# Attention and experts on one core: wavelength weights folded into the row sums at the PSUM copy, stores queued behind loads, output bias added early

## The reference, cut to what is computed

```python
xn = layernorm(x)                                   # (16, 256, 128)
Q, K, V = heads(xn @ Wq + bq), heads(xn @ Wk + bk), heads(xn @ Wv + bv)   # 16 heads of 8
for wl in range(16):                                # wavelengths
    m = cos(phase_modulators[wl])                   # one number a head
    s = (Q * m) @ (K * m).T / sqrt(8)
    s = s * cos(2.7e-12 * s * s)
    acc += (softmax(s) @ V) * interference_weights[wl]
attn = (acc / 16) @ Wo + bo
ffn = top-1 routed experts of xn, each with 640 slots: relu(t @ w1 + b1) @ w2 + b2, times the gate's probability
out = x + attn + ffn
```

## Time and profile before

| | us |
|---|---|
| median of 3 runs (all: 1810.4, 1809.99, 1807.09) | 1809.99 |
| the profiled execution, its own time | 1809.65 |
| its span, first to last instruction | 1807.9 |
| ScalarE busy in the span | 1726.9 (96%) |
| VectorE busy | 1526.0 (84%) |
| TensorE busy | 1490.7 (82%) |
| GpSimd busy | 157.6 (9%) |
| mean granted TensorE clock | 0.986 |

### The profile page before, as it was taken

How to read it: one execution, slowest core, us unless ns; L and a number is a source line. 1 busy time by engine, 2 the same in 40 slices (tenths; PEclk the granted TensorE clock), 3 DMA queues, 4 the chain that set the end, 5 groups by cost and what they waited for, 6 DMA issues and landing times. The chain is left out here.

```text
span 1807.9 us, 45710 instructions
## 1 busy us (share of the span) xinstructions
PE 1490.7 (82%) x20014; PEld 942.5 (52%) x20014; DVE 1526.0 (84%) x2554; ACT 1726.9 (96%) x533; POOL 157.6 (9%) x168
## 2 busy tenths in 40 slices
PE   4797888777899999999997787777787787778877
PEld 2364544544556666656664454444455555445555
DVE  8445887889898888988888999999988998898785
ACT  3699999999999999999999999999999999999995
POOL 6200111110000000000000131332000000000000
PEclk9799999999999999999999999999999999999998
DMA  6000111000011110111000000000000000000001
GB/s 207 21 15 15 37 49 43 23 25 15 22 36 42 42 43 20 31 36 43 22 22 15 18 12 25 23 25 19 15 2 15 15 15 15 15 15 2 8 13 31
DMA packets 44999, 50.07 MB, mean 28 GB/s; under 512 B 6725, under 2 KB 37359, under 8 KB 44799
## 3 DMA queue, kind: packets, MB, share of 16 engines
q1 hardware_dynamic: 42463, 42.91, 7.5%
q0 software_dynamic: 2048, 4.20, 0.7%
q10 hardware_dynamic: 288, 0.00, 0.0%
HBM read 30.96 MB, written 15.73 MB: 26 GB/s over the span
## 5 line engine op out<-in xcount | busy, mean ns | idle before, releaser
L1044 ACT ACTIVATE Pr<-T 128x4096 f32<-128x4096 f32 x482 | 1694.3, 3626 | 17.7 <-PE bank L924 16.9
L924 PE MATMUL bank<-Pr,Vst 128*32 128x256 f32 x15424 | 936.7, 383 | 249.6 <-ACT Pr L1044 140.9
L924 PEld LDWEIGHTS bank<-Pr,Vst 128*32 128x32 f32 x15424 | 520.2, 110 | 546.8 <-issue 343.8
L866 DVE COPY T<-bank 128x512 f32<-128x512 f32 x252 | 172.4, 684 | 82.9 <-PE bank L860 82.9
L850 DVE TENSOR_REDUCE negmax<-bank 128x2 f32<-128x512 f32 x256 | 164.1, 681 | 30.1 <-PE bank L844 28.7
L1015 PE MATMUL bank_b<-terms,ident 128*128 128x128 f32 x1024 | 150.3, 280 | 0.8 <-DVE terms L1003 0.7
L965 DVE SCALAR_TENSOR_TENSOR d_mantissa<-d_mantissa 128x1024 f32<-128x1024 f32 x108 | 147.0, 1361 | 0.0
L968 DVE SCALAR_TENSOR_TENSOR shared<-shared,d_scaled 128x1024 f32<-128x1024 f32 x108 | 140.0, 1297 | 0.0
L1015 PEld LDWEIGHTS bank_b<-terms,ident 128*128 128x128 f32 x1024 | 130.3, 192 | 16.0 <-issue 9.1
L971 DVE SCALAR_TENSOR_TENSOR shared<-d_mantissa,shared 128x1024 f32<-128x1024 f32 x108 | 132.0, 1222 | 2.9
L963 DVE SCALAR_TENSOR_TENSOR shared<-d_mantissa 128x1024 f32<-128x1024 f32 x108 | 130.9, 1212 | 0.0
(11 more groups left out here) (175 smaller groups left out, 911.1 us busy)
## 6 DMA issues: line engine op xcount, KB each, us to landing
Ks<-qk_parts SPq DMA_DIRECT2D x31, 288.0 KB
Qs<-qk_parts SPq DMA_DIRECT2D x93, 96.0 KB
work<-in_L_ffn_w_dram SPq DMA_DIRECT2D x16, 256.0 KB, 3.5
qk_parts<-Pr SPq DMA_DIRECT2D x8, 384.0 KB, 2.7
qk_parts<-work SPq DMA_DIRECT2D x8, 384.0 KB, 2.8
dispatched<-T SPq DMA_DIRECT2D x5, 512.0 KB, 4.9
region<-dispatched SPq DMA_DIRECT2D x8, 320.0 KB, 3.5
expert_out<-work SPq DMA_DIRECT2D x8, 320.0 KB, 2.4
```

Of the source, the lines that this page charges most:

```text
L866: nc.vector.tensor_copy(T[par][:, ds(p * BANK, BANK)], sc_bank[rr][:, :]).then_inc(sc_read, 1)
L924: ins = nc.tensor.matmul(bank[VC * j:VC * (j + 1), half * SEQ:(half + 1) * SEQ], Vst[par][:, at:at + VC], moving, start=opens and half == ...
L1044: nc.scalar.activation(Pr[n % RING][:, :], T[par][:, :], ACT.Exp, scale=scales[u % 2][w]).then_inc(exp_done, 1)
```

## The change

There are four parts.

1. A tile `row_weight` (128 x 6, one column a group) is set to 16 by GpSimd, and 16 DMAs on ScalarE's queue then write the 16 wavelengths' weights to the rows of sums, four partitions each. At the end of the setup VectorE takes its reciprocal, `row_scale`.
2. The copy of a group's bank (`dve_products`) becomes a product with that column of `row_scale`: the value rows are divided by 16, the sums by their weight. The reciprocal of a turned sum then holds the weight already, and the operation that formed `gain` is gone, with one wait of VectorE on itself.
3. In SP's order the loads of units 3 and 4 (for units 5 and 6) are issued ahead of the last store of the unit before. The wait for all stores moves with the last one, behind the loads for unit 6.
4. The four additions of the output bias move from `pool_combine` to the beginning of GpSimd's plain path, behind the staging of the first two units.

```diff
+    FIRST_OF = (0, 3, 6, 8, 11, 14)
+    LAST_OF = (2, 5, 7, 10, 13, 15)
...
-        gain = sb("gain", [P, SLOTS, OTW])
+        row_weight = sb("row_weight", [P, len(FIRST_OF)])
+        row_scale = sb("row_scale", [P, len(FIRST_OF)])
...
                 def _(pool):
+                    pool.memset(row_weight[:, :], float(W)).then_inc(weight_room, 1)
                     pool.memset(one_col[:, :], 1.0).then_inc(root_table, 1)
...
                     act.dma_start(bk_s[:, :], bk.rearrange("(d a) -> d a", a=1)).then_inc(bias_in, 16)
+                    act.wait_ge(weight_room, 1)
+                    for w in range(W):
+                        q = GROUP_OF[w]
+                        row = (w - FIRST_OF[q]) * OC + HD
+                        act.dma_start(row_weight[row:P:VC, q:q + 1], weights.rearrange("(a w) -> a w", a=1)[:, w:w + 1].to_broadcast([GR, 1])
+                                      ).then_inc(row_weight_in, 16)
...
                     link(nc.vector.tensor_copy(flag[:, :], one[:, 3:4]))
+                    dve.wait_ge(row_weight_in, 16 * W)
+                    nc.vector.reciprocal(row_scale[:, :], row_weight[:, :])
...
+            def pool_output_bias(pool):
+
+                pool.wait_ge(xn1_ready, SIDE_TILES)
+                for c in range(CHUNKS):
+                    b = base[:, c * CH:(c + 1) * CH, :]
+                    nc.gpsimd.tensor_tensor(b, b, bo_s[:, :].unsqueeze(1).to_broadcast([P, CH, D]), ALU.add).then_inc(biased, 1)
...
             def pool_combine(pool, c):
 
                 s = slice(c * CH, (c + 1) * CH)
-                nc.gpsimd.tensor_tensor(base[:, s, :], base[:, s, :], bo_s[:, :].unsqueeze(1).to_broadcast([P, CH, D]),
-                                        ALU.add).then_inc(pool_comb, 1)
+                pool.wait_ge(biased, CHUNKS)
                 pool.wait_ge(gathered[c], 16 * CH)
                 nc.gpsimd.tensor_tensor(got[:, s, :], got[:, s, :], over(r[:, 0, s], D), ALU.mult).then_inc(pool_comb, 1)
-                pool.wait_ge(pool_comb, 2 * (c + 1))
+                pool.wait_ge(pool_comb, c + 1)
                 nc.gpsimd.tensor_tensor(base[:, s, :], base[:, s, :], got[:, s, :], ALU.add).then_inc(base_ready, 1)
...
-                nc.vector.tensor_copy(pv_s[q % 2][:, :], pv_bank[q % 2][:, :]).then_inc(pv_copied, 1)
+                nc.vector.tensor_scalar(pv_s[q % 2][:, :], pv_bank[q % 2][:, :], row_scale[:, q:q + 1], None, ALU.mult).then_inc(pv_copied, 1)
...
                 nc.vector.reciprocal(rsum[:, 0:size, :].unsqueeze(3), slots[:, :, :, HD:OC]).then_inc(inverted, 1)
                 dve.wait_ge(inverted, n + 1)
-                nc.vector.tensor_tensor(gain[:, 0:size, :], rsum[:, 0:size, :], weight, ALU.mult).then_inc(gain_ready, 1)
-                dve.wait_ge(gain_ready, n + 1)
                 if n >= 2:
                     dve.wait_ge(terms_summed, n - 1)
                 nc.vector.tensor_tensor(terms[n % 2][:, 0:size, :].rearrange("p s (a d) -> p s a d", d=HD), slots[:, :, :, 0:HD],
-                                        gain[:, 0:size, :].unsqueeze(3).to_broadcast([P, size, OTW, HD]), ALU.mult).then_inc(terms_ready, 1)
+                                        rsum[:, 0:size, :].unsqueeze(3).to_broadcast([P, size, OTW, HD]), ALU.mult).then_inc(terms_ready, 1)
...
                     stage_v(pool, u, u)
+                pool_output_bias(pool)
...
-                for u in range(2, 4):
+                for u in range(2, 5):
                     j = (u - 2) * NQ_SIDE
                     sp.wait_ge(sc_made, pair_no(u, 0))
                     load_stack(sp, u + 2, u % 2)
-                    sp_side1(sp, j, j + NQ_SIDE - 1)
+                    if u > 2:
+                        sp_side1(sp, j - 1, j)
+                    if u < 4:
+                        sp_side1(sp, j, j + NQ_SIDE - 1)
                     load_rows(sp, u + 2, u % 2)
-                    sp_side1(sp, j + NQ_SIDE - 1, j + NQ_SIDE)
-                for u in range(4, EU):
+                for u in range(5, EU):
                     unit(u, u % 2)
```

More of the change, by code:

```diff
@@ L71, in attention_and_experts @@
     RING = 2
+    FIRST_OF = (0, 3, 6, 8, 11, 14)
+    LAST_OF = (2, 5, 7, 10, 13, 15)
+    GROUPS = len(FIRST_OF)
+    GROUP_OF = tuple(sum(w > last for last in LAST_OF) for w in range(W))
     DCOLS = 4 * SEQ
@@ L229, in attention_and_experts @@
             proj, part1, rest1, part2, part3 = (ssem(n) for n in ("proj", "part1", "rest1", "part2", "part3"))
-            v_made = ssem("v_made")
+            v_made, weight_room, row_weight_in = ssem("v_made"), ssem("weight_room"), ssem("row_weight_in")
             angle, sine = ssem("angle"), ssem("sine")
@@ L508, in attention_and_experts @@
                 "v_staged", "exp_done", "pv_done", "pv_copied", "turned"))
-            inverted, gain_ready, terms_ready, terms_summed, summed = (asem(n) for n in (
-                "inverted", "gain_ready", "terms_ready", "terms_summed", "summed"))
+            inverted, terms_ready, terms_summed, summed = (asem(n) for n in (
+                "inverted", "terms_ready", "terms_summed", "summed"))
             exp_table, t0_copied, d_step, whole_done = asem("exp_table"), asem("t0_copied"), asem("d_step"), asem("whole_done")
@@ L518, in attention_and_experts @@
                 "route", "gate_in", "gate_exp", "mask_ready", "index_ready"))
-            scattered, pool_comb, base_ready = asem("scattered"), asem("pool_comb"), asem("base_ready")
+            scattered, pool_comb, base_ready, biased = asem("scattered"), asem("pool_comb"), asem("base_ready"), asem("biased")
             gathered = [asem(f"gathered{c}") for c in range(CHUNKS)]
@@ L994, in dve_turned @@
                 slots = tr_bank[:, :].rearrange("p (a c) -> p a c", c=VC)[:, :, 0:size * OC].rearrange("p a (s c) -> p s a c", c=OC)
-                weight = over(iw_s[:, FIRST_OF[q]:LAST_OF[q] + 1], OTW)
                 dve.wait_ge(turned, n + 1 + 2)
@@ L1048, in stage_v @@
                                       .rearrange("p (t d) -> p t d", d=HD)).then_inc(v_staged, 1)
-            FIRST_OF = (0, 3, 6, 8, 11, 14)
-            LAST_OF = (2, 5, 7, 10, 13, 15)
-            GROUPS = len(FIRST_OF)
-            GROUP_OF = tuple(sum(w > last for last in LAST_OF) for w in range(W))
             COPY_AT = {3: 0, 6: 1, 8: 2, 11: 3, 14: 4, 17: 5}
@@ L1244, in plain_scalar @@
             def plain_scalar(act):
-                nc.scalar.activation(gain[:, 0, 0:1], one_col[:, :], ACT.Exp).then_inc(exp_table, 1)
+                nc.scalar.activation(rsum[:, 0, 0:1], one_col[:, :], ACT.Exp).then_inc(exp_table, 1)
                 for q in range(0, SIDE_B, 2):
```

## The result

The changed kernel takes 1794.97 us (median of 4 runs, 1794.2 to 1795.51), the kernel before 1809.91 beside it (1807.09 to 1810.4): a ratio of 0.992, with a 95% interval from 0.9903 to 0.9938. The forecast was 1796.0, with a range of 1792.5 to 1801.5. The profiled execution took 1794.2 us, its span is 1792.5.

A forecast was written before the change was run, and what follows sets the result against it. ScalarE's exponentials were taken to bound the kernel, so only its waits and the two ends could be won: 1809.65 - 8.0 (loads) - 6.7 (four waits) - 0.3 (end) + 0.2 (reciprocal) + 1.2 (early bias) = 1796.0 us, range 1792.5 to 1801.5.

The forecast's parts named there:

- The base: ScalarE's timeline: the time is its exponentials, the two ends and its waits between, 15 waits of 16.9 us in all.
- Loads ahead of the stores: ScalarE's waits of 3.73 and 4.30 us, at 244.87 and 303.69, go with the earlier loads: 8.0 us less.
- Rival D: The two waits for the loads only shrink, some returning as TensorE's other work; half back gives 1800.0; chance 0.08.
- The four waits: ScalarE's waits in units 17 to 20, where GpSimd's combination holds VectorE: all go, 6.7 us less.
- Rival E: Units 17 to 20: the combination still holds VectorE as long, 2.8 us of waits stay, 1798.8; chance 0.06.
- The fold elsewhere: Gain product dropped outside units 17 to 20: no ScalarE wait there is VectorE's, so nothing for 28 units x 1.0 us.
- The end: Behind the last exponential two groups follow in series, each 0.17 us shorter without the gain product: 0.3 us less.
- The 16 transfers: Setup, ScalarE's queue: 0.45 us each, root ready at 10.4, first root still at 11.01; hidden, 0.6 us spare.
- C: Setup: slow issues on ScalarE's queue, 1.45 us each, the setup slips by up to 15.4 us, 1811.4; chance 0.06.
- The early bias: At the start, GpSimd's four bias operations hold VectorE's cast for unit 1's split until 67.0: 1.2 us more.
- Rival B: At the start, the early bias blocks all of VectorE's first copies and maxima, 9.3 us lost, 1804.1; chance 0.05.
- The sum: Whole kernel: the profiled 1809.65 us with all terms applied gives 1796.0 us, 0.8% less.

The follow-up runs named there:

- loads_only: The kernel before with only SP's new order, the loads for units 5 and 6 issued ahead of the stores; 1800.81 us.
- bias_only: The kernel before with only the output bias added early, weights as before and stores ahead of loads as before; 1802.22 us.
- weights_only: The kernel before with only the weights folded into the bank's copy and their 16 transfers; bias in the combination, stores ahead of loads; 1809.35 us.
- op_twice: The kernel before with loads ahead of stores, bias early behind the 7th exponential, and VectorE's multiplication by the weights made twice in each group; 1793.29 us.
- no_fold: The kernel before with loads ahead of stores and the bias early, but behind the 7th exponential; weights as before; 1793.14 us.
- bias_late: The changed kernel with GpSimd's early bias held back behind the 7th exponential; 1793.26 us.
- weights_late: The changed kernel with the 16 weight transfers on SP's queue and their reciprocal made ahead of the first bank's product; 1793.82 us.
- weights_twice: The changed kernel with 16 more small transfers on ScalarE's queue at the start, into a tensor that nothing reads; 1804.52 us.
- both_late: The changed kernel with the bias behind the 7th exponential and the weight transfers on SP's queue, both together; 1793.38 us.

## Why the prediction was right, step by step

**The base.** "The sum of the exponentials, plus the ends, plus ScalarE's waits" held: 13.55 of the 15.48 us are waits that the rows had named.

**Loads ahead of the stores, -8.0.** The two waits lost 8.03 us in the changed kernel, and loads_only, with nothing else changed, has neither. Rival D is refuted.

**The four waits, -6.7.** They lost 6.71, but the sum behind it gave two reasons, 2.37 us of the bias and 1.0 us of the fold, and only the first was needed: bias_only clears them all, weights_only leaves 5.03 of 6.71, and op_twice adds 0.8 us of VectorE's work to a unit without one. The size of the first was too small: VectorE was held for 6.1 us a unit and is now for 1.9, so that 4.2 us went and not 2.37. I had written that VectorE "falls behind" in units of 52.62 of 55.00 us; that reading of a busy share was the weak one. The other, that it stands while two operations of GpSimd follow each other without a gap, is what the runs bear out: the held time went from 6.1 to 1.9 us with the waits, and in the two units where the step stood for one operation only the waits were 0.45 and 0.90. That the bias in the combination made the waits is shown. Whether the one stretch made them, or the held time added to VectorE's other work, was not told apart; for the stretch speaks weights_only, where 0.7 us less of other work a unit took 0.25 us at most from three of the four. Rival E is refuted.

**The fold elsewhere, nothing; at the end, -0.3.** Elsewhere right, by no_fold: with the gain product (1793.14) the kernel is not slower than without (1793.26 in bias_late). The bank's product costs what was estimated (0.741 us, forecast 0.75):

```profile
L1001 DVE TENSOR_SCALAR pv_s<-bank,row_scale 128x512 f32<-128x512 f32 x192 | 142.3, 741 | 1.1 <-PE bank L944 1.0
```

At the end the fold's worth can be read where the two groups are over, on VectorE's last terms, before and in the changed kernel:

```profile
1791.48 0.42 DVE L1003 TENSOR_TENSOR terms<-bank,gain 128x256 f32<-128x256 f32 x1
```

```profile
1777.01 0.42 DVE L1020 TENSOR_TENSOR terms<-bank,rsum 128x256 f32<-128x256 f32 x1
```

They end 7.33 and 6.92 us behind the last exponential, so it is 0.41 us there. The other traces without the fold have 7.33 or 7.34 (7.55 with the product made twice), those with it 6.92 or 6.93, but for bias_late (7.19).

**The end, -1.42 for -0.3.** The term of the sum that was furthest off. Windows of 3 us, from 6 us behind the last exponential on, with the granted clock as the last number but two, of before, of the changed kernel, and of bias_only:

```profile
1790.60:1793.60 3.00, 2.37 (x13) 1.78 (x10) 1.26 (x4) 0.00 (x0) 0.00 (x0) 0.58 0.02 5
1793.60:1796.60 3.00, 0.00 (x0) 0.00 (x0) 0.00 (x0) 0.00 (x0) 0.00 (x0) 0.50 0.04 8
1796.60:1799.60 3.00, 2.88 (x13) 2.68 (x14) 0.00 (x0) 1.20 (x2) 0.00 (x0) 0.50 0.01 3
```

```profile
1776.50:1779.50 3.00, 1.46 (x11) 1.08 (x10) 1.08 (x3) 0.00 (x0) 0.00 (x0) 1.00 0.02 5
1779.50:1782.50 3.00, 0.77 (x7) 0.80 (x8) 0.00 (x0) 0.10 (x1) 0.00 (x0) 0.99 0.04 11
1782.50:1785.50 3.00, 2.99 (x14) 2.58 (x13) 0.33 (x1) 1.09 (x2) 0.00 (x0) 0.50 0.00 0
```

```profile
1783.40:1786.40 3.00, 1.59 (x12) 1.21 (x10) 1.27 (x4) 0.00 (x0) 0.00 (x0) 1.00 0.02 5
1786.40:1789.40 3.00, 0.31 (x2) 0.34 (x3) 0.00 (x0) 0.00 (x0) 0.00 (x0) 0.89 0.04 11
1789.40:1792.40 3.00, 3.00 (x16) 2.77 (x15) 0.00 (x0) 1.20 (x2) 0.00 (x0) 0.54 0.00 0
```

In before TensorE ran at half its clock (0.58 in the first of these windows, then 0.50 of full, the level of 1.2 GHz), in the changed kernel only in the third. Bias_only, which has no fold, shows the late fall too and an end of 22.19; loads_only shows the early one and 23.42. And weights_late, weights_twice and both_late, which have the fold, show the early one and ends of 23.26 to 23.48. The other 1.0 us of the end thus goes with where the clock falls, not with the fold. The three traces with the late fall (changed, bias_only, weights_only) are each of the shortest run of their kernel, the other eight are not. So the fall may differ from run to run of one kernel, and these 1.0 us may be luck of the runs traced; one trace of each kernel cannot show it. Why the clock falls early or late was not tried.

**The 16 transfers, hidden.** The size was wrong: 0.45 us each was forecast, the rows show 9.14 us for 16, so 0.57; the first alone took 1.10. The spare 0.6 us was overrun, and the first root started at 12.34, not at 11.0: by the text, "if it starts later, C holds". It holds in kind, as weights_twice shows with 9.6 us, but C counted every microsecond of the root's delay. VectorE's first normalisations waited for GpSimd's memsets until about 15 us, with and without the transfers (without them two of the eight were done by 13.2 us and the next two at 15.0 and 15.1, with them the first two at 15.0 and 15.1), and that was cover which the prediction had not seen. The first exponential was 0.27 us later, where the reciprocal's 0.2 us (0.19 measured) was forecast; with a start that varies by 1.07 us without any transfer (last section), that agreement may be luck. One argument against C was misread: ScalarE's issue of 0.45 us was not "at the same moment" as SP's of 1.45, but 4.4 us ahead of it (1.26 and 5.70); the four issues of 1.1 to 1.3 us in weights_twice show that ScalarE's queue has slow ones too.

**The early bias, +1.2.** The wait grew by 1.19 us through the cast that the text named, and bias_late gives it back. Rival B is refuted: the four maxima of VectorE beside the bias took 2.75 us, 0.69 each. The Trainium skill's rule (SBUF — State Buffer, Who interferes with whom: a VectorE instruction with at most one SBUF input, outside the 2-port modes, does not contend) is borne out for additions of two tensors as well: in bias_late the terms, one input in PSUM and one in SBUF, took 0.56 us beside them. The cast has one SBUF input and was held all the same; the rule leaves out the 2-port modes, and no run shows in which mode the cast ran. The same section says that one with two SBUF inputs does contend with a GpSimd instruction that reads SBUF; in bias_only the gain product of two such inputs took 1.41 us beside GpSimd's addition (1077.57 to 1080.82), for 0.20 otherwise:

```profile
1079.47 1.41 DVE L1005 TENSOR_TENSOR gain<-rsum,iw_s 128x32 f32<-128x32 f32 x1
```

**The sum.** 1796.0 forecast, 1794.2 in the profiled execution: 1.1 of the 1.8 us are the end, 0.8 the exponentials themselves with the overlap that the waits had broken. The traced execution was the shortest of four; by the medians, 1809.99 and 1794.97, the gain is 15.0 for 13.65 forecast.

**What beats both kernels.** bias_late, both_late and no_fold lie within 0.25 us of each other, 1.6 to 1.8 us below the changed kernel, and every run of theirs is shorter than its shortest. no_fold has the smallest edit of them: no transfers, no new constant.

## What to carry to other kernels

Where one engine is busy without a gap, price a change by the waits of that engine and by the two ends, one wait at a time: here two of the four parts, a reordered queue and one moved operation, made the whole gain, and the fold, with 192 operations less, made none that a run can tell. An engine that is 95% busy need not be the limit; look for the stretch in which it stands still, and test it by putting work back without the stretch, as much as the stretch had held, and counted by the unit of work, not in a window of fixed length. An operation moved out of the way lands in somebody else's way: ask what runs beside its new place, and move it on until what runs there does not mind.

## What was not expected of the hardware

The first exponential starts between 61.91 and 62.98 us in the five kernels that have the start of the kernel before, 1.07 us apart though their instructions up to there are the same but for bias_only's early bias. In the three with 16 transfers on ScalarE's queue it starts between 63.24 and 63.40. Part of this spread is seen in TensorE's timeline, in the projections of before and of loads_only:

```profile
19.77 1.92 PE L480 MATMUL bank<-xnT,wk_s 128*128 128x512 f32 x2
21.48 1.78 PE L480 MATMUL bank<-xnT,wq_s 128*128 128x512 f32 x2
...
23.53 1.02 PE L480 MATMUL bank<-xnT,wk_s 128*128 128x512 f32 x2
```

```profile
19.79 1.32 PE L480 MATMUL bank<-xnT,wk_s 128*128 128x512 f32 x2
20.94 1.02 PE L480 MATMUL bank<-xnT,wq_s 128*128 128x512 f32 x2
```

The same two products take 1.92 us and later 1.02, and the change comes some 2 us earlier in the one execution than in the other, though the column of the granted clock shows 1.00 from 16 to 28 us in both. What the change of pace comes of was not tried. With such a spread at the start and about 1 us at the end, the single parts do not add up: loads_only, bias_only and weights_only gain 9.1, 7.7 and 0.6 us by their medians, 17.4 together, and the change 15.0. ScalarE's waits show most of the overlap: the three parts take 8.72, 6.61 and 2.23 us from them, 17.56 together, the change 13.55. But 0.67 (loads_only) and 1.68 (weights_only) are of the four waits that the bias's part clears alone, and 0.91 (bias_only) and 0.54 (weights_only) are of the two that the loads' part clears alone; without these 13.76 are left. Of the start and the end, one execution of each kernel was traced, so that what they add to each median stays open.
